# Four graph layers on one core: unnormalised residuals in layers 0 and 1, later masks, zero products, and new orders

## The chip, the cores and the metric

One Trainium2 chip, one of its cores (core 0). The metric is the device time of one execution in microseconds, from its start to its end; lower is better. TensorE is called PE in the rows (PEld is its weight load), VectorE is DVE, ScalarE is ACT, GpSimd is POOL, SyncE is SP; a "q" behind a name is that engine's instruction queue.

## The reference

32 graphs of 256 nodes with 128 features pass through four layers, each followed by a layer norm of the sum of input and layer output. In code, cut to what matters:

```python
# x: (32, 256, 128), adj: (32, 256, 256) of 0 and 1
# layers 0 and 1 (layer 1 has other weights):
h = x @ W.T;  e = leaky_relu(h @ a_src [:, None] + h @ a_dst [None, :], 0.2)
e = where(adj == 0, -huge, e);  x = layernorm(x + softmax(e) @ h, eps=1e-5)
# layer 2, with adj of 0 and 1:
s = leaky((x * a0) @ x.T, 0.2);  alpha = where(adj == 1, sigmoid(s), 0)
x = layernorm(x + alpha @ x + bias2)
# layer 3: x = layernorm(x + (adj @ x) @ W3[0] + bias3)
```

## The kernel before

**Tiling.** Two graphs make a pair (a "team" in the code), so there are 16 pairs, numbered 0 to 15. A graph's 256 nodes are two blocks of 128 partitions. Everything of a pair stays on the chip from its load to its store; the eight banks of PSUM are handed from step to step by a table.

**Orders.** Each engine runs a list written out by hand in `ORDER`: `res0:3` is step `res` of layer 0 for pair 3. Pairs overlap, so an engine works on four or five pairs and several layers at a time. No scheduler changes these lists. `BANKS` says which PSUM bank (one digit per graph, or one for the pair) each product writes. Semaphores tie the lists together: a step waits until the step that makes its input has counted up.

**Steps of layers 0 and 1** (l is the layer). PE: `h` projects x to 130 columns, the last two being the two logit columns (L1115); `dT` and `top` turn and spread the maximum (L1122, L1126); `rows` spreads the gains over the rows (L1133); `out` multiplies the weights by the values (L1176), where a 129th column gives the row sum of the softmax, s. `xT` turns x for the next layer (L1100). ACT: `gains`, `v` and `vals` are exponentials and scaled values (L625, L631, L641), `logits` copies the logit columns (L619, on DVE L830), `seen` checks the mask's values. DVE: `weight` (L856) is the masked maximum, which gives the softmax weights before division; `rsum` reads s out of PSUM (L873 for layer 0, L875 for layer 1, where it is multiplied by the reciprocal deviation of layer 0), `rinv` inverts it (L881), `res` computes the residual out/s + x (L901), `stats` its sums (L909), `var` the variance (L915 for layer 1; layer 0 is on ACT L690, POOL L570 or DVE L919, as the lists say). POOL: `pow` (L540) raises it to the power -1/2, `norm` (L554) or ACT's `norm` (L681, L684) applies it, `fscale` multiplies it into the values' scale.

The residual of layer 0 stays unnormalised between the two layers; the layer norm does not care for a common factor of a row, and the kernel uses that.

**Layers 2 and 3.** PE: `score` (L1143), `out2` (L1176), `agg` (L1153), `out3` (L1173). ACT: `sigmoid` (two of L657/L658 for a graph), `high`, `agg`, `norm2`, `norm3`. DVE: `umax` (L819), `alpha` (L864), `res2`, `res3` (L889), `low` (L792), `norm` (L812). POOL: `bias` (L535), `low` (L546), `xTa` (L564).

**Loads.** SP issues the loads of x and of x turned (`x`, `xT`) and the stores; POOL issues the loads of the masks, `mask:n`, 16 of them, each its own buffer (L519). Mask 6 and later wait for `weight0` of six pairs before.

**Before the first product and at the end.** PE runs seven products of zeros while it waits for the first load (L1184). `centre:0` to `centre:3` on DVE centre the weights and biases; `turn` on PE turns the centred weights of layer 1. `judge` on DVE gathers whether any input lies outside what this fast path allows; its result decides whether a general path runs after it (with these inputs it does not, L961).

**PSUM hand-over.** `freed_by` names the step after which a bank may be written again; PE waits for it in `bank_free`. Before, it is `res0` and `res1` on DVE for the banks of `out0` and `out1`.

## Time and profile before

| what | value |
|---|---|
| time, median of 3 runs | 245.51 us (245.35 to 246.8) |
| the profiled execution: its own time, and its span | 246.51 us, 244.7 us |
| PE busy | 225.0 us, 92% of the span |
| PE weight load busy | 207.1 us, 85% |
| DVE busy | 223.4 us, 91% |
| ACT busy | 188.3 us, 77% |
| POOL busy | 172.9 us, 71% |
| DMA | 17.57 MB, 72 GB/s on average |

The span is what the profiler saw of one execution; what lies around it is 1.8 us in that execution. Busy time is time in which an engine has an instruction under way; instructions that overlap on one engine are counted once.

### The profile page before, as it was taken

The page shows a single profiled execution, that of the slowest core. Times are in us where ns is not written, and L with a number is a line of the kernel's source. Part 1 is how long each engine was busy: PE and PEld are TensorE (multiplying, and loading weights), DVE is VectorE, ACT ScalarE, POOL GpSimd, SP SyncE. Part 2 cuts the span into 40 slices and gives each one's busy share as a digit, 9 for nine tenths or more (in the row PEclk, how much of TensorE's full clock was granted, in tenths as well). Part 3 has the DMA queues.
Part 4 walks back from the last instruction along what each step waited for, and adds up shares of the span by engine and source line. Part 5 has one row for each costly group of instructions (what it writes and reads, how often), then busy time and mean ns, then how long its engine had stood idle before and what let it go on. Part 6 is the DMA issues. An engine that isn't in the chain of part 4 may idle for free.

```text
span 244.7 us, 5718 instructions
## 1 busy us (share of the span) xinstructions
PE 225.0 (92%) x1749; PEld 207.1 (85%) x1749; DVE 223.4 (91%) x747; ACT 188.3 (77%) x603; POOL 172.9 (71%) x262
## 2 busy tenths in 40 slices
PE   7689999999999999999999999999999999989730
PEld 7589899888999998989999998999998988868620
DVE  1838999899999999999999999999999999999980
ACT  2257879788779899899576869958699899778670
POOL 5002516995698789776677978878599988887870
PEclk9959999999999999999999999999999999999955
DMA  7970962433047023002720040004001011000034
GB/s 182 238 244 4 206 184 43 93 126 43 4 136 161 7 87 44 1 0 47 233 83 30 3 129 1 4 1 129 3 0 47 0 44 46 0 0 3 3 129 135
DMA packets 12145, 17.57 MB, mean 72 GB/s; under 512 B 1104, under 2 KB 5968, under 8 KB 12112
## 3 DMA queue, kind: packets, MB, share of 16 engines
q1 hardware_dynamic: 9520, 12.85, 15.8%
q0 software_dynamic: 2304, 4.20, 10.5%
q8 instruction: 15, 0.25, 0.4%
q10 hardware_dynamic: 288, 0.14, 0.2%
q14 instruction: 18, 0.15, 0.2%
HBM read 17.17 MB, written 4.19 MB: 87 GB/s over the span
## 4 chain that ended last, share of the span: by engine, by line
PE 56%; DVE 32%; issue 4%; DMA 2%; POOL 1%; ACT 1%; DVEq 0%
PE banks L1176 25%; PE banks L1115 9%; DVE wgt_all L856 7%; DVE fstats L909 6%; PE banks L1143 6%; DVE fres_all L901 5%; PE banks L1100 4%; PE banks L1133 3%; DVE fres_all L889 3%; PE banks L1173 3%; DVE banks L819 3%; DMA xT_all<-x_turned 2%; DVE wgt_all L864 2%; PE banks L1153 2%; PE banks L1184 1%
## 5 line engine op out<-in xcount | busy, mean ns | idle before, releaser
L540 POOL TENSOR_TENSOR frstd<-fvar,minus_half 128x4 f32<-128x4 f32 x64 | 64.9, 1021 | 17.4 <-DVE fvar L915 6.0
L1176 PE MATMUL banks<-vals_all,wgt_all 128*128 128x129 f32 x512 | 64.3, 280 | 0.6 <-issue 0.6
L1176 PEld LDWEIGHTS banks<-vals_all,wgt_all 128*128 128x128 f32 x512 | 61.3, 196 | 1.5 <-issue 1.0
L856 DVE SCALAR_TENSOR_TENSOR wgt_all<-banks,gain,mask_all 128x256 f32<-128x256 f32 x128 | 52.6, 469 | 0.0
L909 DVE BATCH_NORM_STATS2 fstats<-fres_all 128x6 f32<-128x256 f32 x128 | 47.4, 414 | 0.1
L535 POOL TENSOR_TENSOR xb_all<-xs_all,bias_cen 128x256 f32<-128x256 f32 x60 | 42.3, 728 | 1.1 <-ACT xs_all L684 1.0
L684 ACT ACTIVATE xs_all<-fres_all,frstd 128x128 f32<-128x128 f32 x116 | 37.2, 404 | 2.3 <-POOL frstd L540 2.3
L1176 PE MATMUL banks<-xs_all,wgt_all 128*128 128x128 f32 x256 | 31.8, 277 | 0.5 <-DVE wgt_all L864 0.5
L1176 PEld LDWEIGHTS banks<-xs_all,wgt_all 128*128 128x128 f32 x256 | 29.8, 192 | 1.6 <-DVE wgt_all L864 1.5
L1143 PE MATMUL banks<-fxT,fxTa 128*128 128x256 f32 x128 | 30.4, 381 | 0.3 <-issue 0.3
L611 ACT COPY fxT<-banks 128x256 f32<-128x256 f32 x64 | 20.7, 386 | 7.8 <-PE banks L1100 7.5
L1143 PEld LDWEIGHTS banks<-fxT,fxTa 128*128 128x128 f32 x128 | 22.9, 190 | 3.1 <-issue 0.4
L554 POOL TENSOR_SCALAR xs_all<-fres_all,frstd,fcenter 128x128 f32<-128x128 f32 x48 | 21.0, 450 | 4.7 <-DVE fcenter L923 3.2
L546 POOL TENSOR_TENSOR fxTa<-xs_all,fxTa 128x256 f16<-128x256 f32 x30 | 19.6, 674 | 6.0 <-ACT fxTa L664 6.0
L889 DVE SCALAR_TENSOR_TENSOR fres_all<-banks,xb_all 128x512 f32<-128x512 f32 x32 | 21.6, 675 | 1.3 <-PE banks L1173 1.0
L657 ACT ACTIVATE wgt_all<-banks 128x512 f32<-128x512 f32 x32 | 19.6, 612 | 2.9 <-PE banks L1143 2.7
L819 DVE TENSOR_TENSOR banks<-banks,wgt_all 128x512 f32<-128x512 f32 x32 | 20.8, 685 | 0.3 <-ACT banks L658 0.3
L1115 PE MATMUL banks<-w_fast,xT_all 128*128 128x130 f32 x128 | 18.4, 291 | 2.2 <-DMA xT_all<-x_turned 1.7
L864 DVE SCALAR_TENSOR_TENSOR wgt_all<-banks,mask_all 128x512 f32<-128x512 f32 x32 | 20.4, 676 | 0.0
L658 ACT ACTIVATE banks<-banks 128x512 f32<-128x512 f32 x32 | 19.8, 618 | 0.0
L1133 PE MATMUL banks<-ident,gain 128*128 128x128 f32 x128 | 19.1, 275 | 0.2 <-ACT vals_all L641 0.2
L641 ACT ACTIVATE vals_all<-banks,fscale 128x128 f32<-128x128 f32 x64 | 18.3, 375 | 0.9 <-DVE fscale L846 0.4
(93 smaller groups left out, 409.0 us busy)
## 6 DMA issues: line engine op xcount, KB each, us to landing
xT_all<-x_turned SPq DMA_DIRECT2D x16, 256.0 KB, 3.7
mask_all<-adj_turned POOLq DMA_DIRECT2D x16, 256.0 KB, 5.2
x_all<-x_laid SPq DMA_DIRECT2D x16, 256.0 KB, 3.9
out<-xs_all SPq DMA_DIRECT2D x16, 256.0 KB, 2.2
bias<-biases_laid SPq DMA_DIRECT2D x1, 128.0 KB, 6.3
w_pack<-W_and_columns ACTq DMA_DIRECT2D x1, 68.0 KB, 2.9
w_fast<-W_turned ACTq DMA_DIRECT2D x1, 64.0 KB, 3.2
w_nat<-in_L_gnn_W SPq DMA_DIRECT2D x1, 64.0 KB, 5.1
```

The lines of the kernel that those rows point to most:

```text
L535: nc.gpsimd.tensor_tensor(xb(u)[:, :, :], xs(u)[:, :, :], bias_cen[:, int(l) - 2, :, :], ALU.add).then_inc(fast_pool[k], 1)
L540: nc.gpsimd.tensor_tensor(frstd[:, int(l), slot(n), :], fvar[:, int(l), slot(n), :], minus_half[:, :, :], ALU.pow).then_inc(fast_pool[k], 1)
L684: last = nc.scalar.activation(xs(u)[:, b, :], fres(u)[:, b, :], ACT.Copy, scale=frstd[:, int(l), u, b:b + 1])
L819: nc.vector.tensor_tensor(scored, scored, wgt(u), ALU.max).then_inc(fast_dve[k], 1)
L856: last = nc.vector.scalar_tensor_tensor(out=wgt(u)[:, c, :], in0=place(f"rows{l}", u), scalar=gain[:, u, c, 1:2], in1=maskT(u)[:, c, :], o ...
L864: nc.vector.scalar_tensor_tensor(out=wgt(u), in0=scored, scalar=1.0, in1=maskT(u), op0=ALU.add, op1=ALU.mult).then_inc(fast_dve[k], 1)
L889: nc.vector.scalar_tensor_tensor(out=fres_all[:, pair(n, FRES), :, :], in0=gathered, scalar={"2": 0.5, "3": 1.0}[l], in1=xb_all[:, pair(n, ...
L909: nc.vector.bn_stats(fstats[:, u, :, :].rearrange("p b k -> p (b k)"), fres(u)[:, :, :].rearrange("p b d -> p d b")).then_inc(fast_dve[k], 1)
L1115: last = nc.tensor.matmul(place(f"h{l}", u)[:, b * HC:(b + 1) * HC], (xT_in if l == "0" else fxT)(u)[:, b * P:(b + 1) * P], w_fast[:, int( ...
L1133: last = nc.tensor.transpose(place(f"rows{l}", u)[:, b * P:(b + 1) * P], gain[:, u, b, 0:1].to_broadcast([P, P]), ident[:, :])
L1143: last = nc.tensor.matmul(place("score", u)[:, c * N:(c + 1) * N], fxTa(u)[:, c * P:(c + 1) * P], fxT(u)[:, :], start=True, stop=True)
L1176: last = nc.tensor.matmul(place(f"out{l}", u)[:, b * width:(b + 1) * width], wgt(u)[:, c, b * P:(b + 1) * P], (vals if l in "01" else xs)( ...
```

## The change

Six things are changed together.

1. The residuals of layers 0 and 1 are kept times the row sum: where s is the row sum, `res0` is now s * x + out instead of out/s + x. The reciprocals (`rinv`) go, and so does layer 0's `rsum`: DVE reads s straight from PSUM as the scalar of the residual. Layer 1's `rsum` stays and its product s * (reciprocal deviation) is used as the scalar.
2. The small constant of the variance then has to be times s squared. A new step `sq` on ACT squares sqrt(eps) * s out of PSUM into `fsq`, once for each pair and layer, as one instruction if the pair's two banks are neighbours, else as two. `var` of layers 0 and 1 is one DVE instruction that adds `fsq`; it is never on ACT or POOL any more. Both columns of layer 1's logit weights lose their factor sqrt(eps).
3. The bank of `out0` and `out1` is free after `sq` and no longer after `res`; `sq` waits for `res`.
4. The loads of masks 3, 4 and 5 wait for pair 2's projection `h0:2`.
5. Two gaps of PE get products of zeros: `warm:6` ahead of `h0:4` (six) and `warm:7` ahead of `agg:13` (seven). Each waits first until the bank of the step behind it is free.
6. All five order lists and the bank table are new.

By instructions on the fast path: DVE loses 32 reciprocals and 22 row-sum reads of layer 0, and has 32 two-input variances (`fvar<-fstats,fsq`) instead of 16 (`fvar<-fstats,fvar`), 5 plain ones instead of 10, 21 `fsum` instead of 18, 8 norm instructions instead of 12, 4 `low` instead of 2, and two more small ones in `judge`. ACT gains 44 squares, 8 norm instructions and has 18 variances instead of 24 and 16 `xTa` instead of 18. POOL has 9 variances instead of 14, 44 norm instructions of layer 1 instead of 48, 16 `xTa` instead of 14, 28 `low` instead of 30. PE has 20 zero products instead of 7.

The core of the diff:

```diff
-TINY = 1e-30
+SQUARE_FLOOR = 1e-25
+VARIANCE_CAP = 1e30
 ORDER = {
     "sp": (
-        "xT:1 xT:0 weights:0 xT:2 weights:1 xT:4 weights:2 xT:3 x:0 x:2 x:1 xT:6 xT:7 x:4 xT:5 x:3 x:6 xT:8 x:5 x:7 xT:9 "
+        "xT:1 xT:0 xT:2 weights:0 xT:4 weights:1 xT:3 x:2 weights:2 x:0 x:1 xT:7 x:4 x:5 x:6 xT:6 x:3 x:8 xT:5 x:7 xT:9 "
...
     "pe": (
-        "h0:0 h0:1 rows0:0 dT0:1 turn:0 dT0:0 rows0:1 top0:1 top0:0 h0:2 dT0:2 h0:4 out0:0 dT0:4 top0:2 rows0:2 out0:1 "
+        "h0:1 h0:0 rows0:1 dT0:1 h0:2 dT0:0 dT0:2 top0:1 top0:2 top0:0 rows0:0 rows0:2 turn:0 warm:6 h0:4 out0:2 dT0:4 "
...
+        "out3:15 agg:11 out3:11 agg:14 warm:7 agg:13 out3:14 out3:13"
...
             def cast_mask(l, n, k):
                 if n >= AHEAD:
                     pool.wait_ge(fast_dve[(n - AHEAD) % K], at("dve", "weight0", final(n - AHEAD)))
+                elif n >= 3:
+                    pool.wait_ge(fast_pe[2 % K], at("pe", "h0", final(2)))
...
+            def squares(l, n, k):
+                act.wait_ge(fast_dve[k], at("dve", f"res{l}", final(n)))
...
+                for us, view in pieces:
+                    sums = view[:, :, 0:NB * (D + 1)].rearrange("p u (b c) -> p u b c", b=NB)[:, :, :, D]
+                    last = nc.scalar.activation(fsq[:, int(l), us, :], sums, ACT.Square, scale=math.sqrt(EPS))
+                last.then_inc(fast_act[k], 1)
...
-                    if l == "0":
-                        last = nc.vector.tensor_scalar(frow[:, us, :], sums, TINY, None, ALU.max)
-                    else:
-                        last = nc.vector.scalar_tensor_tensor(out=fsum[:, us, :], in0=sums, scalar=TINY, in1=frstd[:, 0, us, :],
-                                                              op0=ALU.max, op1=ALU.mult)
+                    last = nc.vector.tensor_tensor(fsum[:, us, :], sums, frstd[:, 0, us, :], ALU.mult)
...
-            def inverses(l, n, k):
-                dve.wait_ge(fast_dve[k], at("dve", f"rsum{l}", n * H))
-                nc.vector.reciprocal(finv[:, slot(n), :], frow[:, slot(n), :] if l == "0" else fsum[:, slot(n), :]).then_inc(fast_dve[k], 1)
...
                     for b in range(NB):
-                        last = nc.vector.scalar_tensor_tensor(out=fres(u)[:, b, :], in0=sums[:, b, 0:D], scalar=finv[:, u, b:b + 1],
-                                                              in1=(x_in if l == "0" else fres)(u)[:, b, :], op0=ALU.mult, op1=ALU.add)
+                        last = nc.vector.scalar_tensor_tensor(out=fres(u)[:, b, :], in0=(x_in if l == "0" else fres)(u)[:, b, :],
+                                                              scalar=sums[:, b, D:D + 1] if l == "0" else fsum[:, u, b:b + 1],
+                                                              in1=sums[:, b, 0:D], op0=ALU.mult, op1=ALU.add)
...
-                if l == "1":
-                    nc.vector.scalar_tensor_tensor(out=var, in0=squares, scalar=1 / D, in1=fvar[:, 0, slot(n), :],
+                if l in "01":
+                    dve.wait_ge(fast_act[k], at("act", f"sq{l}", n * H))
+                    nc.vector.scalar_tensor_tensor(out=var, in0=squares, scalar=1 / D, in1=fsq[:, int(l), slot(n), :],
...
-                        "rows0": (fast_dve, "dve", "weight0"), "out0": (fast_dve, "dve", "res0"),
+                        "rows0": (fast_dve, "dve", "weight0"), "out0": (fast_act, "act", "sq0"),
...
-                        "rows1": (fast_dve, "dve", "weight1"), "out1": (fast_dve, "dve", "res1"),
+                        "rows1": (fast_dve, "dve", "weight1"), "out1": (fast_act, "act", "sq1"),
```

**The head of PE's list**, before: the names are the tiles written and read; `wgt_all` holds softmax weights, `xT_all` loaded x turned, `w_cen` the centred weights of layer 1.

```order
L1133 MATMUL banks<-ident,gain 128x128 x4
L1122 MATMUL banks<-ident,logit 4x128
L1061 MATMUL banks<-ident,w_cen 128x128
L1062 MATMUL banks<-w_pack,w_cen 128x2
L1122 MATMUL banks<-ident,logit 4x128
L1133 MATMUL banks<-ident,gain 128x128 x4
L1126 MATMUL banks<-ident,top 128x4 x2
L1115 MATMUL banks<-w_fast,xT_all 128x130 x4
L1122 MATMUL banks<-ident,logit 4x128
L1115 MATMUL banks<-w_fast,xT_all 128x130 x4
L1176 MATMUL banks<-vals_all,wgt_all 128x129 x8
```

and now, from the first `rows` on:

```order
L1144 MATMUL banks<-ident,gain 128x128 x4
L1133 MATMUL banks<-ident,logit 4x128
L1126 MATMUL banks<-w_fast,xT_all 128x130 x4
L1133 MATMUL banks<-ident,logit 4x128 x2
L1137 MATMUL banks<-ident,top 128x4 x3
L1144 MATMUL banks<-ident,gain 128x128 x8
L1072 MATMUL banks<-ident,w_cen 128x128
L1073 MATMUL banks<-w_pack,w_cen 128x2
L1195 MATMUL banks<-zero 128x128 x6
L1126 MATMUL banks<-w_fast,xT_all 128x130 x4
L1187 MATMUL banks<-vals_all,wgt_all 128x129 x8
```

Pair 2's projection moved ahead of the maxima, three pairs' rows stand ahead of the first `out0` instead of two, and the six zero products stand between them and pair 4's projection.

**DVE around the residuals**, before, from the eighth softmax-weight step on:

```order
L873 TENSOR_SCALAR frow<-banks 128x4
L838 TENSOR_REDUCE top<-banks 4x1
L881 RECIPROCAL finv<-frow 128x4
L846 TENSOR_TENSOR fscale<-vals_all,frstd 128x4
L901 SCALAR_TENSOR_TENSOR fres_all<-banks,finv,x_all 128x128 x4
L875 SCALAR_TENSOR_TENSOR fsum<-banks,frstd 128x4
L842 TENSOR_REDUCE minus_dmax<-banks 128x1
L881 RECIPROCAL finv<-fsum 128x4
L909 BN_STATS fstats<-fres_all 128x6 x2
L901 SCALAR_TENSOR_TENSOR fres_all<-banks,finv,fres_all 128x128 x4
```

and now, at the first residual of layer 1:

```order
L882 TENSOR_TENSOR fsum<-banks,frstd 128x4
L848 TENSOR_REDUCE top<-banks 4x1
L852 TENSOR_REDUCE minus_dmax<-banks 128x1
L905 SCALAR_TENSOR_TENSOR fres_all<-fres_all,fsum,banks 128x128 x4
L914 BN_STATS fstats<-fres_all 128x6 x2
L856 TENSOR_TENSOR fscale<-vals_all,frstd 128x4
L921 SCALAR_TENSOR_TENSOR fvar<-fstats,fsq 128x4
```

The reciprocal between the row sum and the residual is gone, and the variance reads what ACT wrote.

**ACT's list in the head**, now, with the squares of pairs 2, 1 and 0:

```order
L699 ACTIVATE fsq<-banks 128x4
L612 COPY fxT<-banks 128x256 x2
L604 ACTIVATE odd_square,odd<-mask_all,minus_half 128x1024
L626 ACTIVATE gain<-logit 128x8
L604 ACTIVATE odd_square,odd<-mask_all,minus_half 128x1024
L626 ACTIVATE gain<-logit 128x8
L699 ACTIVATE fsq<-banks 128x2 x2
L612 COPY fxT<-banks 128x256 x2
L699 ACTIVATE fsq<-banks 128x2 x2
L612 COPY fxT<-banks 128x256 x2
```

Before, no instruction of ACT read the row sums; each of these waits for the residual of its pair, and what stands behind it waits with it.

## Rows read from the trace of the kernel before

**Rows 1.** Page, parts 1 and 4: busy time of each engine, and the chain by engine.

```profile
PE 225.0 (92%) x1749; PEld 207.1 (85%) x1749; DVE 223.4 (91%) x747; ACT 188.3 (77%) x603; POOL 172.9 (71%) x262
...
PE 56%; DVE 32%; issue 4%; DMA 2%; POOL 1%; ACT 1%; DVEq 0%
```

**Rows 2.** Table of windows: busy us of PE, PEld, DVE, ACT, POOL; clock; DMA.

```profile
12.00:13.00 1.00, 0.00 (x0) 0.00 (x0) 0.59 (x4) 1.00 (x4) 0.06 (x1) 0.50 1.08 328
...
20.00:230.00 210.00, 205.91 (x1639) 190.26 (x1639) 205.97 (x677) 174.68 (x559) 162.40 (x243) 1.00 0.22 57
80.00:100.00 20.00, 19.89 (x165) 18.30 (x163) 19.88 (x68) 18.72 (x64) 17.20 (x25) 1.00 0.17 41
180.00:200.00 20.00, 20.00 (x162) 18.90 (x161) 19.89 (x61) 18.91 (x61) 18.87 (x29) 1.00 0.08 27
234.00:235.00 1.00, 1.00 (x6) 0.89 (x5) 0.66 (x2) 1.00 (x5) 1.00 (x2) 0.50 0.02 4
```

**Rows 3.** Timeline of the head: start us, duration us, engine, line, operation.

```profile
7.62 1.66 DVE L856 SCALAR_TENSOR_TENSOR wgt_all<-banks,gain,mask_all 128x256 f32<-128x256 f32 x4
...
9.20 0.47 DVE L838 TENSOR_REDUCE top<-banks 4x1 f32<-4x128 f32 x2
...
11.99 1.14 ACT L641 ACTIVATE vals_all<-banks,vals_all 128x128 f32<-128x128 f32 x4
...
18.86 0.16 DVE L873 TENSOR_SCALAR frow<-banks 128x4 f32<-128x4 f32 x1 [2.83 <-PE banks L1176]
...
19.46 1.12 DVE L901 SCALAR_TENSOR_TENSOR fres_all<-banks,finv,x_all 128x128 f32<-128x128 f32 x4
...
23.14 1.13 DVE L901 SCALAR_TENSOR_TENSOR fres_all<-banks,finv,x_all 128x128 f32<-128x128 f32 x4
```

**Rows 4.** Chain of the head: start us, duration us, what.

```profile
7.17 6.05 DMA xT_all<-x_turned
13.36 2.07 PE banks L1115 x8
15.43 3.39 PE banks L1176 x16
...
31.82 1.78 PE banks L1176 x16
```

**Rows 5.** Groups by line and form: busy us, mean ns, idle before.

```profile
L1184 PE MATMUL banks<-zero 128*128 128x128 f32 x14 | 3.4, 432 | 1.1 <-DVE zero L737 1.1
...
L690 ACT ACTIVATE fvar<-fstats 128x4 f32<-128x4 f32 x24 | 5.1, 213 | 4.2 <-DVE fstats L909 4.2
...
L915 DVE SCALAR_TENSOR_TENSOR fvar<-fstats,fvar 128x4 f32<-128x4 f32 x16 | 3.8, 240 | 0.0
...
L812 DVE TENSOR_SCALAR xs_all<-fres_all,frstd 128x128 f32<-128x128 f32 x12 | 3.6, 358 | 0.7 <-POOL frstd L540 0.7
...
L881 DVE RECIPROCAL finv<-fsum 128x4 f32<-128x4 f32 x16 | 2.6, 164 | 0.0
...
L873 DVE TENSOR_SCALAR frow<-banks 128x4 f32<-128x4 f32 x10 | 1.5, 146 | 2.8 <-PE banks L1176 2.8
L619 ACT COPY logit<-banks 128x8 f32<-128x8 f32 x8 | 1.4, 177 | 3.1 <-PE banks L1115 3.1
```

**Rows 6.** Chain inside a stretch where DVE sets it.

```profile
130.05 0.07 DVE frow L873
...
132.62 0.08 DVE finv L881
```

**Rows 7.** Timeline of DVE and of POOL around 95 us.

```profile
95.17 0.94 DVE L915 SCALAR_TENSOR_TENSOR fvar<-fstats,fvar 128x4 f32<-128x4 f32 x1
...
94.67 1.41 POOL L535 TENSOR_TENSOR xb_all<-xs_all,bias_cen 128x256 f32<-128x256 f32 x2
```

**Rows 8.** Chain of the tail.

```profile
233.37 1.83 PE banks L1173 x8
...
237.06 1.02 POOL frstd L540
```

More of the change, by code:

```diff
@@ L934, in judge @@
[L934 removed]
+                nc.vector.tensor_reduce(bad[:, 2:3], logit[:, :, :, :, :].rearrange("p l u b k -> p (l u b k)"), AX.X, ALU.min)
+                nc.vector.tensor_reduce(bad[:, 3:4], fsq[:, :, :, :].rearrange("p l u b -> p (l u b)"), AX.X, ALU.min)
+                nc.vector.tensor_reduce(bad[:, 4:5], fvar[:, 0, :, :].rearrange("p u b -> p (u b)"), AX.X, ALU.max).then_inc(bad_step, 1)
@@ L1206, in _ @@
             pe.wait_ge(bad_step, 3)
-            nc.tensor.matmul(banks[0:1, 0, 0:1], bad[:, 8:9], ones_col[:, :], start=True, stop=True).then_inc(bad_summed, 1)
+            nc.tensor.matmul(banks[0:1, 0, 0:1], bad[:, 10:11], ones_col[:, :], start=True, stop=True).then_inc(bad_summed, 1)
             def transpose_x(g, l):
```

45 lines of the change are left out of this document (25 added, 20 removed), and 188 rows, old and new, of tables (BANKS, ORDER).

## The prediction

> **What bounds the kernel now.** Read the page's busy row first, then its chain: PE is busy 92% and DVE 91% of the span, and the chain of what ended last lies 56% on PE and 32% on DVE [rows 1]. So neither engine alone is the bound; the chain changes between them. The table of windows says where: from 20 to 230 us PE is busy 205.91 of 210 us and DVE 205.97, at the full clock (1.00, which is 2.4 GHz), while ACT has 174.68 and POOL 162.40 [rows 2]. Of each of the two, only 4 us in that stretch are free. The 35 us that are left are the head up to 20 us and the tail from 230 us, and both have loose time. In the head the chain goes through a load, the transfer of x turned for pair 4, 6.05 us from 7.17 us on; then h0:4 takes 2.07 us and the first out0 3.39 us, where a later out takes 1.78 [rows 4]: at 12 us the granted clock is 0.50, that is 1.2 GHz, and PE does nothing in that window [rows 2]. DVE's first residual starts only at 19.46 us and the second at 23.14 [rows 3]. In the tail the clock is again 0.50 at 234 us [rows 2], and an out3 takes 1.83 us on the chain [rows 8].
>
> **Head.** The DMA queues hold masks 5 and 4 ahead of the load that PE waits for; now these two and mask 3 are issued after h0:2, and the load of pair 2 goes out ahead of a weight. The load of pair 4 is then no longer what h0:4 waits for. What is late next: the six zero products wait for the values of pair 0 on ACT (the bank of h0:4), these for the largest value from DVE. Before, DVE needs from 7.62 to 9.28 us for one weight step and then starts its peaks, and ACT starts these values at 11.99 and is through 1.14 us later [rows 3]. Now three peaks and a centring stand in between: the values are done at about 12.9. Six zero products take 6 x 0.22 = 1.3 us if a product takes an eighth of an out's 1.78 us [rows 4], or 2.9 us at the 0.48 us each of the seven at the start (3.36 us; 14 records of the group, two each) [rows 5]. At the full clock h0:4 then ends at 12.9 + 1.3 + 1.0 = 15.2 and the first out0 at 17.0; its residual starts at 17.2 instead of 19.46. Behind it PE has h0:3, a turn and the second out0 (1.0 + 0.4 + 1.8, and the turn waits for the residual's 1.12 us), so the second residual starts at 20.8 instead of 23.14. But DVE has then not made the sums of the first (0.7 us), so DVE is ahead by 2.3 - 0.7 = 1.6 us, PE by about as much. The four constants' steps move behind the first residual; the wait for the second out0 covers their 2 us, and without that cover they cost them. At the low clock the same walk gives 12.9 + 2.9 + 2.0 = 17.8, and the second residual at about 23.3: a loss of 0.5 us. What PE does between 7 and 12 us is no more than before, and before the clock was down at 12 us; against it the zero products are there to bring it back. I take **-0.9 us**, ends -1.7 and +0.5.
>
> The Trainium skill ("TensorE: Matmul & The Clock Gate", section "What's actually happening") says that TensorE falls to half its clock after an idle stretch and comes back after a busy one, so that products of zeros can hold it up. The window at 12 us agrees (PE busy 0.00, clock 0.50). It speaks against half of this change: the products stand behind the wait for ACT and fill no idle time before it.
>
> **DVE.** Out go 32 reciprocals and 22 row-sum reads. They last 0.164 and 0.146 us [rows 5], but where DVE sets the chain they follow other work at 0.07 to 0.08 us [rows 6]: 54 x 0.08 = 4.3 us. In come 16 two-input variances (32 instead of 16). The group of that form has a mean of 240 ns, and without hold-ups such small instructions last 0.15 [rows 5], as the reciprocals and row sums show. The longest took 0.94 us: it started at 95.17 and ended at 96.11, just as POOL's pair of additions, 94.67 + 1.41 = 96.08, was over [rows 7]. So each costs its 0.07 plus 0.09 of being held up: 16 x 0.16 = 2.6 us. The rest: five plain variances fewer, -0.4; three `fsum` more, +0.2; a norm of four instructions off DVE, which by their mean of 358 ns is up to -1.4, by their pace where they are dense about -0.9 [rows 5]; one `low` pair more, taken as +0.8, since it is two instructions of 256 elements, longer than those of 128; two more small ones in `judge`, +0.2. Together -4.3 + 2.6 - 0.4 + 0.2 - 0.9 + 0.8 + 0.2 = **-1.8 us**. Ends: -3.2 if POOL never holds a variance up; 0 if PE, which is as busy and loses nothing, keeps the pace.
>
> The Trainium skill ("GPSIMD Engine Reference", section "8. Key points") has it that GpSimd shares its SBUF interfaces with VectorE and that they contend when a VectorE instruction has two SBUF inputs; the new variance has two and the ones that leave ACT had none of this. The rows agree (0.94 us beside POOL's 1.41). Without that rule the same 16 would cost 16 x 0.07 = 1.1 us.
>
> **The way through a pair.** From the end of out0 the old kernel went row sum, reciprocal, residual: it started at 18.86 and the residual at 19.46, so 0.60 us [rows 3]; now the residual itself is what waits for PE, and layer 1 has one hop less. That is up to 0.6 us for layer 0 and 0.3 for layer 1, in each of 16 pairs, but five pairs are under way at once and the engines have other work in it, so it is on the path only where a queue's head waits for it. The ends are 0 and 16 x 0.9 / 5 = -2.9 us; I take **-0.8**, nearer to 0, as only 4 us of each engine's time are free in the middle.
>
> **Squares and banks.** 44 squares go to ACT. The nearest row is the copy of as many elements out of PSUM, 177 ns; six variances of 213 ns leave it [rows 5]: 44 x 0.177 - 6 x 0.213 = +6.5 us, and eight norms less two scalings add some 2. ACT has 35 us free between 20 and 230, so this is covered nearly everywhere; from 80 to 100 and from 180 to 200 it has only 1.3 and 1.1 us free [rows 2], and there 8.5 x 20/210 = 0.8 us more nearly fills it. Each square waits at ACT's head for its residual, and everything behind it on ACT waits too: values, sigmoids, copies for PE. A bank of out is free one square later, 0.18 us or more, and the variance needs the square. I take **+0.4 us**, ends 0 and +2 (what is over in the full windows, and a few late banks).
>
> **Tail.** The last out3 at the full clock would take 0.9 instead of 1.83 us [rows 8]. The seven zero products (1.5 us, or 3.4 at the low clock) lie in a wait of PE for the low part of pair 13; if that cover is gone they delay agg:13 by themselves. **-0.6**, ends -0.9 and +1. The last power on POOL, 1.02 us, stays [rows 8].
>
> **Masks.** Masks 3 to 5 are wanted after the first residuals, from 20 us on; issued at 9 us instead of 3 to 5 they still have over 10 us. POOL's queue behind them held masks and the first variance, nothing that is due.
>
> **Sum.** -0.9 - 1.8 - 0.8 + 0.4 - 0.6 = -3.7 us. Against the profiled execution, 246.51 us, that is 242.8. This execution lay 1.0 us above the median of the runs, 245.51; so the forecast is **241.8 us**.
>
> **Rivals.**
> *The head gives nothing.* The clock is down at 12 us and the zero products run at half speed: +0.5 for -0.9, and the tail likewise 0 for -0.6. For it speaks that PE does no more between 7 and 12 us than before. 245.51 - 1.7 = 243.8 us. Chance 0.18.
> *The scalar out of PSUM costs.* 64 residual instructions of layer 0 now read a scalar from PSUM beside a PSUM tensor; no row shows that. If each pays what one more small PSUM read costs in a dense row, 0.07 us [rows 6], that is +4.5 us, and the sum is +0.8: 246.3 us. Against it: reads of PSUM and of SBUF last alike (0.146 and 0.164 us) [rows 5]. Chance 0.10.
> *ACT becomes the third bound (slower).* A square stands at the head of ACT's queue until its residual is made, and holds up the values and copies that PE needs. ACT has 35 us free in the middle [rows 2]; they are used up from the point where a square with its wait takes 35 / 44 = 0.8 us of ACT, and in the full windows, 80 to 100 and 180 to 200, earlier. At 1.0 us each it is 44 - 35 = +9 us, less the 4.1 of the other terms: +4.9, so 250.4 us. For it speaks that ACT is 94% busy in those windows; against it that a square alone is 0.18 us and the lists can place it late. Chance 0.14.
> *The change does not do what it says:* PE's load of pair 4 lands as late because the x loads now crowd it. With +0.5 for the head's -0.9 and the rest as it is, 243.2 us; it is in the first rival's chance.
>
> **How the numbers follow.** The forecast's own case has 0.58, with its range from 238 to 243.5. The range that should hold 8 of 10 goes from 237.5 (head -1.7, DVE -3.2, way -2, tail -0.9, less 1.0 for the median, rounded) to 247.0, which takes in the first two rivals and leaves out most of the third. One per cent, 2.5 us, is about what a measurement of this kernel can tell from no change. Faster by over 1% (under 243.05): most of the own case and a little of the first rival, 0.58. Within 1%: 0.26. Slower: 0.16.
>
> **What would show it.** Right: the first residual near 17 us and the window at 12 to 16 us with clock 1.00; DVE busy in all some 2 us less, the variances' mean near 240 ns; residuals of both layers still at 0.34 us; ACT busy near 197 us. Wrong: clock 0.50 through 18 us; residuals of layer 0 at 0.40 us; waits of PE on ACT's fsq, or of DVE's fvar on it; ACT 99% busy in a window. The forecast fails most easily by the orders: the lists are new from end to end, and in a stretch with 4 us free on both engines a list can lose or find more than any term above.

## The result, and the profile after

The changed kernel takes 247.97 us, median of 19 runs (245.22 to 250.05); the kernel before takes 244.91 us on the same chips (19 runs, 243.92 to 247.86). The ratio is 1.010, 95% interval 1.0076 to 1.0125: **slower by 1%**, 2.5 us, where 3.7 us less was forecast. The ratio leaves out the few executions in the chip's slower state, so it is a little smaller than that of the two medians, which lie 3.1 us apart. The profiled execution took 247.29 us, span 245.5.

Parts 1 and 4 of its page, the answer to [rows 1]:

```profile
PE 225.3 (92%) x1775; PEld 208.7 (85%) x1775; DVE 220.2 (90%) x707; ACT 193.8 (79%) x647; POOL 171.5 (70%) x253
...
PE 66%; DVE 22%; ACT 5%; issue 3%; POOL 2%; DVEq 0%
```

DVE is busy 3.3 us less than before (223.4 to 220.2), ACT 5.5 us more, PE as much as before: its products are the same, and it has 13 zero products more. The chain has moved from DVE (32% to 22%) to PE (56% to 66%). So what DVE was spared is there, and the time has still risen. PE's work is given, so the time is that work plus what PE waits, and the windows say where (columns as in [rows 2]):

```profile
12.00:13.00 1.00, 0.94 (x8) 0.69 (x7) 0.96 (x7) 0.51 (x3) 0.00 (x0) 1.00 1.05 256
...
20.00:230.00 210.00, 202.85 (x1618) 187.68 (x1617) 202.57 (x642) 179.51 (x599) 159.20 (x231) 1.00 0.21 55
80.00:100.00 20.00, 19.88 (x165) 18.37 (x163) 18.70 (x59) 17.58 (x60) 12.92 (x17) 1.00 0.22 59
180.00:200.00 20.00, 20.00 (x168) 18.82 (x167) 18.60 (x66) 18.47 (x67) 16.16 (x25) 1.00 0.09 29
234.00:235.00 1.00, 1.00 (x10) 0.88 (x8) 0.71 (x2) 1.00 (x5) 0.84 (x1) 1.00 0.00 0
```

At 12 us and at 234 us the clock is now 1.00 where [rows 2] have 0.50, as forecast. But from 20 to 230 us PE is busy 202.85 us, where it was 205.91, and DVE 202.57 where it was 205.97. Each now has some 7 us free in that stretch instead of 4, although one of them has less to do. The changed kernel enters the window 2 us ahead of this execution of before (first residuals below) and ends its last out3 level with it, at 235.08 against 235.18 us: that lead is what the added waiting uses up.

The head, timelines of DVE and then of PE (start, duration, engine, line, what):

```profile
17.56 0.62 DVE L905 SCALAR_TENSOR_TENSOR fres_all<-x_all,banks 128x128 f32<-128x128 f32 x2 [0.73 <-PE banks L1187]
18.45 0.61 DVE L905 SCALAR_TENSOR_TENSOR fres_all<-x_all,banks 128x128 f32<-128x128 f32 x2 [0.28 <-PE banks L1187]
...
21.06 1.24 DVE L905 SCALAR_TENSOR_TENSOR fres_all<-x_all,banks 128x128 f32<-128x128 f32 x4
```

```profile
14.06 1.60 PE L1195 MATMUL banks<-zero 128*128 128x128 f32 x12
15.50 1.06 PE L1126 MATMUL banks<-w_fast,xT_all 128*128 128x130 f32 x8
16.40 1.95 PE L1187 MATMUL banks<-vals_all,wgt_all 128*128 128x129 f32 x16
```

The first residual starts at 17.56 (forecast 17.2, before 19.46 [rows 3]), the second at 21.06 (forecast 20.8, before 23.14). The six zero products (two records each) take 1.60 us ahead of h0:4, in this execution at the full clock.

Groups of DVE and ACT, the answer to [rows 5] and [rows 7] (busy us, mean ns):

```profile
L905 DVE SCALAR_TENSOR_TENSOR fres_all<-x_all,banks 128x128 f32<-128x128 f32 x64 | 18.9, 344 | 2.4 <-PE banks L1187 2.1 <-ACT fxT L612 0.2
L905 DVE SCALAR_TENSOR_TENSOR fres_all<-fres_all,fsum,banks 128x128 f32<-128x128 f32 x64 | 17.7, 333 | 0.0
...
L921 DVE SCALAR_TENSOR_TENSOR fvar<-fstats,fsq 128x4 f32<-128x4 f32 x32 | 6.1, 195 | 0.0
...
L699 ACT ACTIVATE fsq<-banks 128x4 f32<-128x4 f32 x20 | 3.6, 179 | 1.2 <-DVE fres_all L905 1.2
...
L699 ACT ACTIVATE fsq<-banks 128x2 f32<-128x2 f32 x24 | 2.9, 181 | 4.4 <-DVE fres_all L905 4.4
```

The residual of layer 0 with its scalar out of PSUM lasts 344 ns (341 before), that of layer 1 333. The variance with two inputs has a mean of 195 ns over 32, not 240. A square lasts 180 ns.

Waits (us in total, times, longest):

```profile
POOL frstd L541 <- DVE fvar L921: 24.4, 12, 9.8
...
ACT fsq L699 <- DVE fres_all L905: 5.6, 10, 1.3
...
PEld banks L1187 <- DVE wgt_all L874: 3.8, 4, 1.7
...
PE banks L1187 <- DVE wgt_all L874: 2.9, 4, 1.3
...
PEld banks L1126 <- ACT fsq L699: 0.4, 2, 0.2
```

PE hardly waits for squares (0.4 us); it waits for the weights of layer 2 that DVE makes (L874, 3.8 + 2.9 us). POOL's 24 us cost nothing by themselves, POOL has room; only at the very end is POOL on the chain (below). Two places near the end, in PE's and in DVE's timeline:

```profile
212.45 2.02 PE L1187 MATMUL banks<-xs_all,wgt_all 128*128 128x128 f32 x16 [1.32 <-DVE wgt_all L874]
...
230.69 1.73 PE L1195 MATMUL banks<-zero 128*128 128x128 f32 x14
```

```profile
209.94 0.17 DVE L940 TENSOR_REDUCE bad<-odd 128x1 f32<-128x16 f32 x1 [1.69 <-ACT banks L659]
```

DVE's judge stands 1.69 us for ACT, and PE then waits 1.32 us for the weights of pair 11; and the seven zero products lie directly ahead of the sums of pair 13, on the chain. Both are suspects, tried below.

The end, in POOL's and in DVE's timeline, of the kernel before and then of the changed one. `frstd` is a power on POOL, `redo_i` the last instruction of DVE:

```profile
237.06 1.01 POOL L540 TENSOR_TENSOR frstd<-fvar,minus_half 128x4 f32<-128x4 f32 x1 [1.04 <-DVE fvar L919]
239.21 0.15 DVE L961 TENSOR_SCALAR redo_i<-banks 1x1 int32<-1x1 f32 x1 [0.23 <-DVE xs_all L812]
```

```profile
236.41 2.04 POOL L541 TENSOR_TENSOR frstd<-fvar,minus_half 128x4 f32<-128x4 f32 x2
239.99 0.15 DVE L972 TENSOR_SCALAR redo_i<-banks 1x1 int32<-1x1 f32 x1 [0.62 <-DVE xs_all L822]
```

The last out3 ends at 235.18 us before and at 235.08 now; from there to the end of `redo_i` it is 4.18 us before and 5.06 now. Before, POOL stands idle for 1.04 us and then makes one power for the last pair. Now two powers follow each other, and the last pair's waits behind another pair's. All profiles agree: the eight others with the old lists have 4.16 to 4.18 us there, whatever their arithmetic, the eight others with the new lists 5.06 to 6.70. So the new lists lose 0.9 us or more behind the last product.

### The profile page after: what moved, and what is told of

It is laid out like the page before. It is cut to its first block, busy times and chain, and to the rows that moved or that the text cites. A ratio compares the mean times of both kernels' runs of the same rounds, so it can differ in the third digit from the quotient of the medians.

```text
span 245.5 us, 5803 instructions
## 1 busy us (share of the span) xinstructions
PE 225.3 (92%) x1775; PEld 208.7 (85%) x1775; DVE 220.2 (90%) x707; ACT 193.8 (79%) x647; POOL 171.5 (70%) x253
## 4 chain that ended last, share of the span: by engine, by line
PE 66%; DVE 22%; ACT 5%; issue 3%; POOL 2%; DVEq 0%
PE banks L1187 27%; PE banks L1126 10%; PE banks L1154 6%; PE banks L1111 5%; DVE wgt_all L866 5%; PE banks L1144 5%; PE banks L1164 4%; PE banks L1184 4%; DVE banks L829 3%; DVE wgt_all L874 3%; DVE fstats L914 3%; PE banks L1195 3%; DVE fres_all L905 2%; POOL frstd L541 2%; DVE fres_all L891 2%
## 5 line engine op out<-in xcount | busy, mean ns | idle before, releaser
L1187 PE MATMUL banks<-vals_all,wgt_all 128*128 128x129 f32 x512 | 62.6, 276 | 1.2 <-DVE wgt_all L874 0.8
L1187 PEld LDWEIGHTS banks<-vals_all,wgt_all 128*128 128x128 f32 x512 | 59.8, 191 | 2.1 <-DVE wgt_all L874 1.0
L685 ACT ACTIVATE xs_all<-fres_all,frstd 128x128 f32<-128x128 f32 x120 | 38.0, 405 | 1.9 <-POOL frstd L541 1.7
L612 ACT COPY fxT<-banks 128x256 f32<-128x256 f32 x64 | 20.8, 387 | 2.4 <-PE banks L1111 2.4
L547 POOL TENSOR_TENSOR fxTa<-xs_all,fxTa 128x256 f16<-128x256 f32 x28 | 18.2, 672 | 6.3 <-ACT fxTa L665 6.3
L555 POOL TENSOR_SCALAR xs_all<-fres_all,frstd,fcenter 128x128 f32<-128x128 f32 x44 | 19.2, 452 | 3.2 <-DVE fcenter L929 2.6
L905 DVE SCALAR_TENSOR_TENSOR fres_all<-x_all,banks 128x128 f32<-128x128 f32 x64 | 18.9, 344 | 2.4 <-PE banks L1187 2.1
L874 DVE SCALAR_TENSOR_TENSOR wgt_all<-banks,mask_all 128x512 f32<-128x512 f32 x32 | 20.4, 676 | 0.0
L1126 PE MATMUL banks<-w_fast,xT_all 128*128 128x130 f32 x128 | 19.1, 297 | 0.5 <-DVE w_fast L767 0.5
```

What stands on the lines that cost most here:

```text
L685: last = nc.scalar.activation(xs(u)[:, b, :], fres(u)[:, b, :], ACT.Copy, scale=frstd[:, int(l), u, b:b + 1])
L874: nc.vector.scalar_tensor_tensor(out=wgt(u), in0=scored, scalar=1.0, in1=maskT(u), op0=ALU.add, op1=ALU.mult).then_inc(fast_dve[k], 1)
L905: last = nc.vector.scalar_tensor_tensor(out=fres(u)[:, b, :], in0=(x_in if l == "0" else fres)(u)[:, b, :], scalar=sums[:, b, D:D + 1] if ...
L1126: last = nc.tensor.matmul(place(f"h{l}", u)[:, b * HC:(b + 1) * HC], (xT_in if l == "0" else fxT)(u)[:, b * P:(b + 1) * P], w_fast[:, int( ...
L1187: last = nc.tensor.matmul(place(f"out{l}", u)[:, b * width:(b + 1) * width], wgt(u)[:, c, b * P:(b + 1) * P], (vals if l in "01" else xs)( ...
```

## Experiments

Ratios are to the kernel before, run beside each, with 95% intervals. "New lists" are the changed kernel's lists and banks, "old lists" those of before.

### Arithmetic and lists, crossed

```diff
 # a: old arithmetic, new lists
-ACT  ... sq0:2 xT1:2 ... sq1:0 ...
+ACT  ... xT1:2 ...
-DVE  ... res0:2 ... rsum1:0 ... res1:0
+DVE  ... rsum0:2 rinv0:2 res0:2 ... rsum1:0 rinv1:0 ... res1:0
 # b: new arithmetic, old lists
-DVE  ... rsum0:0 dmax0:2 rinv0:0 peak0:4 res0:0 ... stats0:0 rinv0:1 dmax0:4 ...
+DVE  ... dmax0:2 peak0:4 res0:0 ... stats0:0 dmax0:4 var0:0 ...
-ACT  ... vals0:2 seen:4 ...
+ACT  ... vals0:2 sq0:0 seen:4 ...
```

> The old arithmetic (row sum, reciprocal, scaled residual in layer 0; reciprocal in layer 1; plain variance of layer 0; the old judge) in the changed kernel's lists and banks: the squares are taken out of ACT's list, the row sum and the reciprocal of a pair stand right ahead of its residual, masks and zero products as in the changed kernel. Theory L (the new lists and banks lose what the arithmetic saves): the old arithmetic adds its price to the changed kernel, 247.4 + 3 to 4 = about 251 us, ratio to before 1.02 to 1.03. Theory S (the squares on ACT and the longer hold of the banks are what costs): without them the lists show their own worth, the head's 1.5 to 3 us, so 242 to 245, ratio 0.99 to 1.00.

> The new arithmetic in the old lists and banks: 32 reciprocals and 16 row sums leave DVE's list, the variance of layer 0 stands on DVE where it stood in time, each square stands in ACT's list where ACT was in the trace of before when the residual ended, the judge two steps after the last pair's centre of layer 1 (it needs the last square); no zero products in the gaps, masks 3 to 5 without their wait. Theory L: the arithmetic alone is worth its terms, -1.8 and -0.8 and +0.4 and a little for lists that were not made for it, so 242 to 243.5 us, ratio 0.988 to 0.995. Theory S: slower than before, ratio 1.00 to 1.02.

Measured: a 1.0479 (1.0416 to 1.0542), b 1.0745 (1.0698 to 1.0792). Neither theory alone holds: each arithmetic is good only in its own lists (1.000 and 1.010) and bad in the other's. So the crossed pair says little of either part; it says that arithmetic and lists that were not made for each other cost 9 us (a, over the changed kernel) and 18 us (b, over before), more than any term of the forecast. In b the waits show one mechanism:

```profile
PEld banks L1110 <- ACT fsq L698: 8.0, 8, 1.9
PEld banks L1125 <- ACT fsq L698: 6.3, 6, 1.7
PE banks L1110 <- ACT fsq L698: 5.6, 6, 1.5
...
PE banks L1125 <- ACT fsq L698: 4.9, 6, 1.3
```

PE stands for squares again and again: the old table hands a bank of out on as soon as the residual has read it, and now a square in ACT's queue comes between.

### What the banks cost: squares on DVE, and squares without banks

```diff
 # f, on b: the read that makes the square on DVE, bank free after res
+nc.vector.tensor_scalar(fsq[...], sums, math.sqrt(EPS), 0.0, ALU.mult, ALU.max)
-"out0": (fast_act, "act", "sq0")
+"out0": (fast_dve, "dve", "res0")
 # g, on before: 44 squares in ACT's list, of a constant
+act.wait_ge(fast_dve[k], at("dve", f"res{l}", final(n)))
+nc.scalar.activation(fsq[...], minus_half[...], ACT.Square, ...)
```

> As the new arithmetic in the old lists and banks (1.0745), but the read of the column of sums that makes the square stands on DVE, in the place of the old row sum in layer 0 and of the old reciprocal in layer 1 (it writes the scaled sum, not its square, so the output differs a little), and DVE's residual gives a bank of out free, as in the kernel before. Theory B (what costs 7 per cent there is that a bank of out waits for a square in ACT's queue): back to before, ratio 0.995 to 1.01. Theory V (it is the variance of layer 0 on DVE, or another place in the list): still 1.04 or more.

> The kernel before, with 44 squares of the same shape added in ACT's list where the new arithmetic in the old lists has them: each waits for the pair's residual, but reads a constant and writes a tensor that nobody reads, so that no bank and no variance waits for it. Theory B (banks wait for the squares): the squares cost only ACT's time, 44 x 0.18 us in 35 us that are free, ratio 1.000 to 1.010. Theory of the third rival (ACT's queue stands at its head and holds up copies for PE): 1.02 to 1.06.

Measured: f 1.0197 (1.0162 to 1.0232), g 1.0046 (1.0025 to 1.0067). f meets neither of its two expectations; it lies between them. Of b's 7.5%, some 5.5 go with the square's way to ACT (the late bank, ACT's own time and what waits behind the square, together); the other 2 stay with the row sums' reads and the variance of layer 0 on DVE, which this run doesn't part. Squares that hold no bank and no variance cost 1.1 us, although ACT has 35 us free: more than the forecast's 0.4, far from the third rival's 9.

### What DVE is spared, and what more costs

```diff
 # e, on before: 54 instructions out of DVE's list
-rsum0:n rinv0:n ... rinv1:n
-scalar=finv[:, u, b:b + 1]
+scalar=sums[:, b, D:D + 1] if l == "0" else fsum[:, u, b:b + 1]
 # k, on before: each reciprocal twice
+nc.vector.reciprocal(fspare[...], ...)
 # n, on the changed kernel: row sums, centres, variances of layer 0 twice
+nc.vector....(fspare[...], ...)
```

> The kernel before with nothing moved, less the 54 small instructions on DVE that the change removes: no reciprocals in either layer, no row-sum read in layer 0; the residual of layer 0 takes its scalar out of PSUM, that of layer 1 takes the row sum where the reciprocal stood (so the output isn't the reference's), and the judge reduces half of the layer 1 sums in place of the row sums. Theory P (from 20 us on PE is full and sets the time; what DVE is spared buys nothing): within 1 us of before, ratio 0.996 to 1.002. Theory of the prediction (54 x 0.08 = 4.3 us less on DVE, and up to 0.6 us of way for each pair): 3 to 5 us less, ratio 0.980 to 0.988.

> The kernel before with each of its 32 reciprocals issued twice (the first of the two into a tensor that nobody reads), nothing else moved. Theory E (the lists stand at an edge: less on DVE buys nothing, since PE is full, but more on DVE costs in full, since DVE is as full): 32 x 0.08 to 0.16 us = 2.6 to 5.1 us more, ratio 1.010 to 1.020. Theory P in its plain form (PE alone sets the time and DVE has slack): ratio 1.000 to 1.003.

> The changed kernel with 53 small instructions of DVE issued twice, the first of the two into a tensor that nobody reads: 21 row sums and 16 centres of layer 1 and 16 variances of layer 0. Theory E (the new lists hold DVE at an edge, and it is the number of DVE's instructions that made the old arithmetic cost 3.8 per cent in them): 4 to 10 us more than the changed kernel, ratio to before 1.026 to 1.05. Theory W (it was the longer way, row sum and reciprocal ahead of each residual that PE waits for): as in the old lists, 0.03 us each, 1 to 2 us more, ratio 1.013 to 1.019.

Measured: e 0.9988 (0.9960 to 1.0016), k 1.0039 (1.0004 to 1.0074), n 1.0204 (1.0165 to 1.0243). In e DVE is busy 220.0 us, 3.4 less than before, the same relief as in the changed kernel, with nothing else moved (it leaves out the division by the row sum, so its output is not the reference's), and **the time stays**. Windows of e:

```profile
12.00:13.00 1.00, 0.90 (x8) 0.70 (x7) 1.00 (x4) 0.06 (x2) 0.00 (x0) 1.00 1.07 359
20.00:230.00 210.00, 204.83 (x1631) 189.06 (x1630) 203.09 (x625) 174.69 (x561) 163.71 (x246) 1.00 0.21 56
```

DVE is free 6.9 us there instead of 4.0; PE is free 5.2 us instead of 4.1, but the window now takes in 2 us more of the tail. Steps of e follow those of before at a constant distance: 2.0 us ahead at the end of the first out0 and 2.2 at the last one. These 2.0 us come from the clock of the head (below); the other 0.2 are all that 54 instructions gave on the way to it. More on DVE costs 0.03 us an instruction in the old lists by the ratios (32 for 0.0039 x 245) and 0.05 in the new (53 for 0.0104 x 245); compared at like clock (below) it is 0.05 in both. So theory E, the edge, asked too much, and k lies above what the plain form of theory P gave, n between its two: taking work off DVE gives nothing, putting more on it costs part of it. The rest of a's 9 us over the changed kernel is then not the number of DVE's instructions; its row sums wait 4.6 us for PE (L877, 8 times, longest 1.5). That the longer way costs the rest is likely, but no run shows it by itself.

### Head: zero products, clock, masks, loads

```diff
 # h, on before                       # i, on the changed kernel
-PE ... h0:4 ...                      -PE ... warm:6 h0:4 ...
+PE ... warm:6 h0:4 ...               +PE ... h0:4 ...
+elif n >= 3: pool.wait_ge(fast_pe[2], at("pe", "h0", final(2)))
 # o: h without warm:6; on SP xT:2 ahead of weights:0, xT:4 of weights:1, xT:3 of weights:2
 # p, on the changed kernel
-elif n >= 3: pool.wait_ge(fast_pe[2], at("pe", "h0", final(2)))
```

> The kernel before with the six zero products ahead of the products of pair 4 and masks 3 to 5 behind the products of pair 2, and nothing else. Theory H (the head's gain is lost again, as PE and DVE are full behind it and hold each other): the first residuals 1 to 2 us earlier, the time within 1 us of before, ratio 0.997 to 1.003. If the head's gain reaches the end: 1.5 to 2.5 us less, ratio 0.990 to 0.994. If the load of pair 4's x turned still comes late and the products only add to it: 1.003 to 1.008.

> The changed kernel without the six zero products ahead of the products of pair 4. Theory Z (the clock is up there in most executions without them, and they stand on PE's path by themselves, 1.0 to 1.6 us): 0.5 to 1.2 us less than the changed kernel, ratio to before 1.006 to 1.009. If the clock falls without them and the first outputs run at half of it: 1 to 2 us more, ratio 1.015 to 1.02.

> The kernel before, unchanged, for a second profile of it. If the fall of the clock at 12 us is a matter of the execution and not of the kernel: the clock stands at 1.00 from 9 us to the tail, the first residual starts near 17 us and the second near 21, and the span is 242 to 243.5 us. If it belongs to the kernel: 0.50 at 12 us again, and 244 to 245.

> The kernel before with masks 3 to 5 behind the products of pair 2 and the load of pair 2's x turned ahead of the first weight, no zero products. If the loads were what the head waited for (0.3 to 1.7 us ahead of the products of pair 4 in the profiles): 0.5 to 1 us less, ratio 0.996 to 0.998. If the head waits for DVE's and ACT's steps of the first pairs anyway: 0.999 to 1.001. If the first weight, now later, makes PE's turn of it late: 1.002 to 1.006.

> The changed kernel without the wait of masks 3 to 5 for the products of pair 2. If the wait is worth its place (the load of pair 4 waits behind masks without it): 0.5 to 2 us more, ratio to before 1.012 to 1.018. If it changes nothing, since the zero products wait for ACT anyway: 1.009 to 1.011. If the wait itself costs: 1.006 or less.

Measured: h 1.0050 (1.0014 to 1.0085), i 1.0071 (1.0032 to 1.0110), o 0.9988 (0.9954 to 1.0021), p 1.0143 (1.0099 to 1.0187). The second profile of the kernel before, windows, and PE's rows of the run without squares (it has the zero products):

```profile
12.00:13.00 1.00, 1.00 (x7) 1.00 (x7) 1.00 (x6) 0.00 (x0) 0.00 (x0) 0.50 1.07 276
20.00:230.00 210.00, 205.27 (x1634) 189.61 (x1633) 205.96 (x676) 174.55 (x558) 161.85 (x242) 1.00 0.22 57
```

```profile
14.59 2.91 PE L1185 MATMUL banks<-zero 128*128 128x128 f32 x12
```

Four things follow. First, the low clock at 12 us is a matter of the execution. Both profiles of the kernel before had it, once with PE busy 0.00 and once with PE busy 1.00 in that window, which by itself was what l expected if it belonged to the kernel. But of the seven variants in which PE has the same steps up to 12 us, b, e, g, h and o had 1.00 there, f and k 0.50. The mean clock of an execution tells it without a profile: of the 18 profiled ones all nine with 0.984 or more have 1.00 at 12 us, and of the nine with less all but b have 0.50. In 93 executions of the kernel before, 55 have 0.983 or more and a mean span of 242.8 us, 22 have 0.971 or less and 244.5 us, the 16 between 244.3. The profile that the forecast rests on has 0.963: it is not of the usual kind.

Second, the profiles show what PE did before it. PE's rows in g, which kept the clock, and in l, which did not, with the window from 7 to 11 us of each:

```profile
5.15 3.80 PE L1128 MATMUL banks<-w_fast,xT_all 128*128 128x130 f32 x16 [0.48 <-DVE w_fast L770]
7.00:11.00 4.00, 3.98 (x23) 3.65 (x21) 1.98 (x8) 0.58 (x3) 0.00 (x0) 1.00 1.13 212
```

```profile
4.95 2.02 PE L1115 MATMUL banks<-w_fast,xT_all 128*128 128x130 f32 x16 [0.48 <-DVE w_fast L757]
9.36 0.30 PE L1061 MATMUL banks<-ident,w_cen 128*128 128x128 f32 x1 [1.84 <-DVE w_cen L748]
7.00:11.00 4.00, 1.50 (x13) 1.02 (x11) 2.54 (x10) 0.38 (x2) 0.00 (x0) 1.00 1.10 208
```

The sixteen records of the first two projections take 3.80 us in the one and 2.02 in the other, although the clock's column says 1.00 in both: there the durations tell more than the column. In all nine profiles with some 3.8 us PE is busy 3.28 to 4.00 us from 7 to 11, and the clock holds; in the nine with 2.02 us PE is through early and then idle, busy 1.50 to 2.96 us of the four, and the clock falls between 11 and 12 us in eight of them (o, 2.40 us, keeps it). So in the profiles it is a fast start with a wait behind it that goes with the fall. What decides how the start runs is not shown.

Third, six zero products do not hold this clock: where they are in the lists and it falls (j, n), it has fallen before they start, at 14.59 and 13.13 us. There they run at half of it, 2.91 us, and in j it is back at 17.6 us, as in l without them. Fourth, they stand on PE's path: without them the changed kernel is 0.3% nearer to before (i against the result, intervals overlap), with them before is 0.5% slower (h, clear of 1). The later masks are worth up to 0.4% in the new lists (p, intervals overlap); with three loads moved as well they give the old ones 0.1%, which is nothing that can be told (o).

A ratio mixes executions with and without the fall, and their shares differ from set to set (5 of 12 of h have a mean clock of 0.982 or more, 23 of the 29 of before beside it). So here are the mean spans of those with 0.982 or more alone, with the kernel before beside each; the last column is two standard errors:

| run | span, us (number) | before (number) | difference | +- |
|---|---|---|---|---|
| the changed kernel | 245.8 (17) | 242.8 (55, all) | +3.0 | 0.5 |
| e, less on DVE | 242.6 (10) | 242.8 (23) | -0.2 | 0.5 |
| g, squares without banks | 243.7 (5) | 242.8 (23) | +0.9 | 0.4 |
| h, zero products, old lists | 243.0 (5) | 242.8 (23) | +0.2 | 0.4 |
| i, none in the head, new lists | 245.1 (7) | 242.7 (14) | +2.4 | 0.3 |
| j, no squares | 245.5 (8) | 242.7 (14) | +2.8 | 0.5 |
| k, reciprocals twice | 244.4 (9) | 242.7 (14) | +1.7 | 0.3 |
| m, no squares, no zero products | 243.5 (8) | 243.1 (11) | +0.4 | 0.4 |
| n, more on DVE, new lists | 248.5 (3) | 243.1 (11) | +5.4 | 0.5 |
| p, masks early, new lists | 246.2 (5) | 243.1 (11) | +3.1 | 0.9 |

This is what "at like clock" means below and above. What e and m say stays. The 0.5% of h does not: most of it is the clock, and the zero products' own price in the old lists is 0.2 us, within its error. k is dearer, 1.7 us or 0.05 an instruction. The masks of p are worth nothing that can be told.

The Trainium skill ("TensorE: Matmul & The Clock Gate", section "What's actually happening") has the clock fall after idle time and come back with activity. The profiles agree with the fall: PE was idle more in the executions that fell, and its 1.00 at 12 us in l came behind the fall. Whether products of zeros in that idle time would hold the clock was not tried, since none of these stands there.

### Tail and judge

```diff
 # c                                  # d
-PE ... agg:14 warm:7 agg:13 ...      -DVE ... center1:13 judge:0 alpha:11 ...
+PE ... agg:14 agg:13 ...             +DVE ... judge:0 res3:14 ...
```

> The changed kernel without the seven zero products ahead of the sums over neighbours of pair 13. If these stand on the path by themselves (the trace shows them from 230.85 us on, 1.56 us, just ahead of agg:13): 1.0 to 1.4 us less than the changed kernel, ratio to before 1.005. If what they bring back is the clock of the tail: the two last out3 and the sums at half the clock, 1 to 2 us more, ratio 1.015. If they lie in a wait that is there anyway and the clock is up without them: no change, 1.010.

> The changed kernel with DVE's judge moved from behind the centre of pair 13 to just ahead of the layer 3 residual of pair 14, where DVE waits for PE 1.03 us. Where it stands now DVE is 3.37 us without work on a pair, a wait for ACT among it, and PE waits 1.32 us for the weights of pair 11. If this gap is carried to the end: 1 to 2 us less than the changed kernel, ratio to before 1.002 to 1.006. If what is behind it waits for other work anyway: no change, 1.010; if the new place is on the path: up to 1 us more, 1.014.

Measured: c 1.0107 (1.0066 to 1.0149), d 1.0128 (1.0087 to 1.0169). Neither is clear of the changed kernel, but their profiles say more. (Profiles of two executions that start alike can be compared closely: in p the last out3 ends at 235.07 us, in the changed kernel at 235.08.) In c the missing products do save PE's time: the aggregation before their place starts 0.81 us later than in the changed kernel (230.63 against 229.82), the one behind it 0.29 us earlier (231.96 against 232.25). That is 1.1 us, and only 0.29 us of a wait stands where they stood. But POOL's last two powers start no earlier (236.62 against 236.41), and they set the end. So the seven products cost nothing only because POOL ends later anyway.

In d the gap was carried: d is 0.48 us behind at 203 us (the same out2 starts at 203.72 and at 203.24) and 1.06 ahead at the last out3:

```profile
232.07 1.95 PE L1186 MATMUL banks<-w_cen,fxT 128*128 128x128 f32 x16
```

That is 1.5 us for the judge's place. They are lost again where d puts it: ahead of the residual of pair 14 it stands in DVE's way to the end, which is 6.70 us from the last out3's end to that of `redo_i`, where the changed kernel has 5.06. So d does not clear the judge. In the kernel before it stands at 203.21 us and waits 0.53 us for ACT; the new one waits for the last squares too, so it comes later.

### Squares, and what is left

```diff
 # j: no squares; m: no squares, no warm:6, no warm:7
-ACT ... sq0:2 ... sq1:0 ...
+nc.vector.memset(fsq[:, :, :, :], EPS)
-"out0": (fast_act, "act", "sq0")
+"out0": (fast_dve, "dve", "res0")
```

> The changed kernel without the squares: ACT makes none, the variances of layers 0 and 1 read a constant in their place (so the output differs a little from the reference's), and a bank of out is free when DVE's residual is done. Theory Q (the squares cost in these lists what they cost in the old ones without their banks, 1.0 us, and the lists give their banks slack): ratio to before 1.004 to 1.008. Theory B (in these lists too the banks wait for them): 2 to 4 us less than the changed kernel, ratio 0.995 to 1.003. If ACT has room for all of them: 1.010 to 1.013.

> The changed kernel without the squares (as in the run without them) and without the zero products of head and tail. If the two prices add, 1.0100 - 0.005 - 0.003 = 1.002 of before: then the new lists with all that DVE is spared are worth nothing, plus or minus 0.5 us. If what DVE is spared shows once ACT's part is gone: 0.985 to 0.995. If the lists themselves lose: 1.005 or more.

Measured: j 1.0049 (1.0009 to 1.0089), m 1.0025 (0.9993 to 1.0056). Taken alone, squares cost 0.5% in the new lists (1.2 us) and the zero products of the head 0.3% (0.7 us), each with an interval nearly as wide. Both together (m) are clear of the changed kernel, 1.8 us less, and as large as the sum, 1.0100 - 0.0051 - 0.0029 = 1.0020 (at like clock m is 2.6 us under the changed kernel, more than j and i together, so the split between the two stays open). The table of windows of m:

```profile
20.00:230.00 210.00, 202.67 (x1616) 187.18 (x1615) 203.04 (x640) 175.77 (x556) 160.34 (x232) 1.00 0.20 53
```

With squares and zero products gone, PE still has 7.3 us free from 20 to 230, as in the changed kernel (7.15), against 4.1 to 5.9 in the profiles of before, e, g, h, k and o. Up to the last product that costs m nothing that shows: its last out3 ends at 232.16 us, that of e at 232.30. What m has too much stands behind it, 5.78 us to the end where e has 4.17.

## Why the prediction was wrong, point by point

**The head (-0.9).** The walk was right to 0.4 us (17.56 and 21.06), the step ahead of it was not: "at 12 us the granted clock is 0.50" was taken for the kernel and is a matter of the execution. Against the usual execution of before there is no clock to win: the residuals of g, at the full clock, with the old arithmetic, the old lists and no zero products, start at 17.61 and 21.29, those of e at 17.38 and 20.73, and the changed kernel's at 17.56 and 21.06. Besides, the 1.0 us by which the profiled execution lay above the median was taken off at the end, though it is mostly this same low clock: the gain was counted twice. What is left is the price of the six products, +0.7 us by i (0.6 at like clock), which the forecast had inside its gain.

**DVE (-1.8) and the way through a pair (-0.8).** The ledger of DVE was right in sum (3.3 us less busy) and worth nothing. The failing step is to turn DVE's spared time into time at all; the ends of both terms at 0, "if PE, which is as busy and loses nothing, keeps the pace", were the value. Experiment e gives both together as -0.3 us (-1.0 to +0.4). The window from 20 to 230 had said it: PE busy 205.91 of 210. Only that part of PE's 4 us of waiting that ends with DVE could go, not DVE's own saving.

**Squares and banks (+0.4).** Mechanism right, size too small: +1.1 us without banks (g), +1.2 us in the new lists (j, with an interval down to nearly nothing, and 0.2 us at like clock). The new table gives the banks room (PE waits 0.4 us for squares), the old one doesn't (b).

**Tail (-0.6).** Leaving the seven products out changes nothing (c), but the new tail as a whole costs +0.9. The out3 at half the clock of [rows 8] was again that one execution: in l the same step starts even later, at 233.96, and takes 1.16 us at the full clock, and so do those of e, g and o. In the changed kernel the last out3 runs at the full clock with and without the seven products. "The last power on POOL, 1.02 us, stays" failed: with the new orders it is two powers in a row, and from the last out3 to the end it takes 5.06 us instead of 4.18.

**Orders.** The forecast gave them no term and said that it fails most easily there. With -0.3 for DVE and way, +0.7 for the zero products, +1.2 for squares and +0.9 behind the last product the sum is +2.5 of the 2.5 us. That it closes so well is luck: each of the first three prices has an error of half a microsecond or more, and the 1.5 us at the judge are not in it, so the lists must find about as much elsewhere. m leaves +0.6 (-0.2 to +1.4) for lists, masks and DVE's relief together. Two places where the lists lose are shown, the powers at the end and the judge; what a list with both mended would take is not tried.

**Rivals.** The scalar out of PSUM costs nothing (344 ns, and e has it too). ACT did not become a bound (at most 18.47 of 20 us in the two full windows). The first rival was right that the head gives nothing, at 243.8 still too low, since the other terms were worth nothing either, and its reason, that the clock is down in the changed kernel too, is not what its profile shows. Slower by over 1% had a chance of 0.16, and no rival had this way to it: several small costs, with nothing on the other side.

No version here beats the kernel before by more than the runs can tell. The nearest is o, its own lists with masks 3 to 5 later and three loads earlier, 0.9988 (at like clock 0.6 us less, +- 0.8).

## What to carry to other kernels

Where two engines are both 98% busy in a stretch, take the given work of one plus its waits as the time, and give work spared on the other a value only for waits that end with it; try it first by leaving the work out with nothing moved, as in e. Ask of a clock, a late load or any other odd second in one profile whether the other executions have it: the mean clock of each run shows it, executions of like clock can be compared by themselves, and a gain over the odd one must not be taken off again against the median. Follow a trial's profile past the place that was changed: in c and d the time was won there and lost again at the end, and the ratio alone hid both. Lists written for one arithmetic are a part of it; crossed with another they took 5 to 7% more than the kernel before, so a new arithmetic is judged with its own lists and the lists by what the bound engine waits.

## What was not expected of the hardware

The clock of PE at 12 us is 1.00 in some executions and 0.50 in others that have the same steps up to there. It goes with how the first two projections ran, 3.80 or 2.02 us for the same sixteen records while the clock's column says 1.00 for both, and with PE's idle time behind them. Executions of the kernel before with a low mean clock take 1.7 us of 245 more (242.8 and 244.5). Apart from such a shift two executions are the same step by step: e, whose DVE has 54 instructions fewer, keeps its distance of 2.0 to 2.3 us to before over 165 us. One more small instruction on a DVE that is 98% busy costs about 0.05 us at like clock, not its 0.08 in a dense row, and one less gives nothing.
